# A first scan spread over twelve tiles, a second scan whose last half states and transposes come one tile later, and router steps woven into the gate products

## The chip, the core and the metric

The kernel runs on one core of a Trainium2 chip. The metric is the device time of one execution in microseconds (us), and less is better. TensorE is called PE here (its weight loads PEld), VectorE is DVE, ScalarE is ACT, GpSimd is POOL, and SP is the engine that issues most DMAs.

## What is computed

The input x is 1024 rows of 256 (4 sequences of 256). It passes a feed-forward layer with experts, a state-space scan, and the same feed-forward layer again, each behind a layer norm:

```python
x = x + 0.5 * ffn(layernorm(x))
x = x + ssm(layernorm(x))
x = x + 0.5 * ffn(layernorm(x))

def ffn(x):            # 8 routed experts, top 2 by sigmoid score; 2 shared experts; hidden width 640
    scores = sigmoid(x @ w_router.T)
    w, i = top_k(scores, 2); w = w / w.sum()
    routed = sum over the 2 chosen experts of w * (silu(x @ wg.T) * (x @ wu.T)) @ wd.T
    return routed + the same without a weight for the 2 shared experts

def ssm(x):            # 256 channels, 16 states each
    proj = x @ W_xproj.T; dt = softplus(proj[:256]); B, C = proj[256:272], proj[272:]
    h[t] = exp(dt * A) * h[t-1] + dt * B * x;  y[t] = sum over states of h[t] * C + D * x
```

All arithmetic is in float32.

## The kernel before

The 1024 rows are taken as two halves of 512, and the two feed-forward layers over two halves make four **segments** 0 to 3. A segment has 17 **tiles** of 128 rows, numbered through from 0 to 67 (`LIST`, with S1 = 17, S2 = 34 and S3 = 51 the first tiles of segments 1 to 3). Of the 17, eight are "shared" (the two shared experts, four row blocks each), five are "whole" (routed experts 0 to 4, 128 slots each), and four are "mixed" (four groups of 32 rows, each with an expert of its own, one of which is read from a table). Shared tiles that are in the set `DIRECT` take their input from `xnt`, the transposed normed rows in SBUF. All other tiles fetch 128 rows from DRAM (`xg_rows`) four tiles ahead on SP's queue, and PE turns them two tiles ahead (`rows_of`, L560), after which ACT copies them to `xt` (L786).

Every engine walks one table, `SCHEDULE`, in order. A tile n is done in two steps. `first(n)` issues the ten gate and up products of tile **n+1** (chunks of 128 columns: `gate_up(n+1)` 0 to 4, 4 to 8, and then 8 to 10, which waits until tile n-1 has been evicted). `second(n)` turns the rows of tile n+2 and issues the down product of tile n (L541, L554). On ACT `first` is the tanh of tile n+1 (L768), and for a mixed tile before it the copy of its turned hidden rows; `second` is the copy to `xt` and, for routed tiles, the eviction (L793), and behind it `send_late(n)` sends expert weights (L802). On DVE `first` is `hidden(n+1)` (L1017 and L1021), and `second` is the eviction of a shared tile into `xres` (L1032). `("tiles", a, b)` is both steps for each of a to b-1, and in `("scan", a, b, h)` the half states of scan h are added to each tile.

A **scan** h (one half of 512 rows) has 32 **half states**: 16 states times two blocks of 128 channels. For each, ACT makes the decay (L858, L859), POOL the input `bx` (L981), DVE the scan itself (L1062) and the product with C (L1067), and POOL adds that to the sum in `xnt` (L995). There are two buffers of each kind, one for each channel block. `half_states(first, n, part)` says which of them stand ahead of (part 0) and behind (part 1) tile n's body: two ahead and one behind, with two at the first tile of a scan. `("X1", h)` projects the scan's inputs ahead of it, and `("Y", h)` turns the finished sum back (L738), once the last add is done.

The **router** of a segment is four steps: R1 (logits, 16 matmuls of 32 rows, L694), a copy by DVE and its transpose on PE (`turn_logits`, L596), `route_scores` on DVE (L1103 to L1122, the top two), R2 (two matmuls that count ranks, L703, L704), and `route_rows` on DVE (L1127 to L1167, the place of every row). The step S then scatters rows from POOL (L943), G gathers results (L961), C adds them to `xres` (L1175), and N1, N2 and T are the layer norm (P before a feed-forward layer, A before a scan) and its transposes (L684).

Weights: shared expert 0 comes first on SP's queue; shared expert 1 and routed expert 0 (`EARLY`) follow there in the step "start". Experts 1 to 7 are sent from ACT's queue behind the tiles that `LATE` names. The first mixed tile of segment 0 has every expert in it, so `first_use` lets PE wait for the gate and up weights of all eight before its gate products:

```python
                if kind_of(n) == "mixed":
                    if index_of(n) == 0:
                        for e in range(E):
                            weights_in(e, k)
```

## Time and profile before

| | |
|---|---|
| median of 3 runs | 530.93 us (530.12 to 531.57) |
| the profiled execution | 526.55 us |
| its span, first to last instruction | 524.8 us |
| PE busy | 509.9 us (97%) |
| DVE busy | 324.4 us (62%) |
| POOL busy | 231.3 us (44%) |
| ACT busy | 158.3 us (30%) |
| data moved by DMA | 67.76 MB |

The span is the profiled execution without what lies around it; the execution's own time is 1.75 us longer. Busy shares are over the whole span, while the stages differ: the two scans fill DVE and POOL, and the rest leaves them half idle. In the timeline a row gives start, length, engine, line, operation, names, shape and count of the instructions merged in it, and in brackets the idle time ahead of the first and what ended it. A float32 matmul shows as two passes, so that a chunk with its two halves of the contraction counts as x4.

### The profile page before, as it was taken

To read this page: it belongs to the slowest core of one execution; us is meant where nothing else is said; L and a number is where in the kernel's file an instruction comes from. 1 tells how busy PE (TensorE), PEld (TensorE's weight loads), DVE (VectorE), ACT (ScalarE), POOL (GpSimd) and SP (SyncE) were. 2 spreads that over 40 slices of the span, in tenths; PEclk is the share of its full clock that TensorE was granted. 3 is DMA by queue.
4 is the path that set the end of the run, shared out by engine and by line. 5 is a ranking of instruction groups with operands and counts; after the bars stand their busy time and mean duration, and the time that the engine had idled before them with its cause. 6 is when DMAs were issued, how large, how long until landed. Compare 5 with 4: busy or idle time off the path is not lost.

```text
span 524.8 us, 11147 instructions
## 1 busy us (share of the span) xinstructions
PE 509.9 (97%) x4408; PEld 413.2 (79%) x4409; DVE 324.4 (62%) x658; ACT 158.3 (30%) x336; POOL 231.3 (44%) x208
## 2 busy tenths in 40 slices
PE   7999999999999999899999999999999999999996
PEld 6899997448988888347998889974479999954696
DVE  3742526521665999998698399999867522522225
ACT  1111121222036444453213643554431111122210
POOL 1050100220513999996445389999900650000041
PEclk9999999999999999999999999999999999999999
DMA  7967995931303455540312525545100231210022
GB/s 225 372 245 275 400 397 206 330 97 31 93 23 134 114 134 157 143 139 23 107 56 92 132 94 125 132 145 152 52 12 14 80 102 41 81 40 15 19 62 72
DMA packets 42087, 67.76 MB, mean 129 GB/s; under 512 B 5136, under 2 KB 24848, under 8 KB 42032
## 3 DMA queue, kind: packets, MB, share of 16 engines
q1 hardware_dynamic: 29280, 38.81, 25.7%
q10 hardware_dynamic: 9088, 18.09, 9.3%
q0 software_dynamic: 3664, 10.10, 6.0%
q8 instruction: 37, 0.61, 0.5%
q14 instruction: 18, 0.15, 0.1%
HBM read 48.76 MB, written 18.22 MB: 128 GB/s over the span
## 4 chain that ended last, share of the span: by engine, by line
PE 65%; POOL 12%; DVE 9%; issue 7%; DMA 5%; SPq 1%; POOLq 0%; ACT 0%; DVEq 0%
PE ps L516 29%; PE ps L541 13%; PE ps L531 11%; POOL region L981 8%; PE ps L554 7%; POOL xnt L995 4%; DVE ps L1062 3%; DMA bcb<-bc_rows 2%; PE ps L565 2%; DMA w_gu<-in_su 1%; PE ps L560 1%; DMA bc_rows<-hh 1%; DVE hb L1017 1%; PE ps L684 1%; DVE xres L1175 1%
## 5 line engine op out<-in xcount | busy, mean ns | idle before, releaser
L516 PEld LDWEIGHTS ps<-xt,w_gu 128*128 128x128 f32 x1360 | 156.6, 192 | 12.6 <-ACT xt L786 4.9
L516 PE MATMUL ps<-xt,w_gu 128*128 128x128 f32 x1360 | 162.3, 277 | 2.5 <-DVE xres L1032 1.5
L1017 DVE SCALAR_TENSOR_TENSOR hb<-hb,ps 128x640 f32<-128x640 f32 x68 | 55.5, 816 | 128.9 <-ACT hb L768 128.7
L541 PE MATMUL ps<-w_dn,hb 128*128 128x256 f32 x520 | 120.7, 379 | 0.0
L541 PEld LDWEIGHTS ps<-w_dn,hb 128*128 128x128 f32 x520 | 94.9, 190 | 10.8
L768 ACT ACTIVATE hb<-ps 128x640 f32<-128x640 f32 x68 | 47.5, 699 | 171.4 <-PE ps L516 157.0
L516 PEld LDWEIGHTS ps<-xnt,w_gu 128*128 128x128 f32 x720 | 82.9, 192 | 1.9 <-issue 1.2
L516 PE MATMUL ps<-xnt,w_gu 128*128 128x128 f32 x720 | 84.1, 276 | 0.2 <-DMA w_gu<-in_su 0.2
L995 POOL TENSOR_TENSOR xnt<-xnt,hh 128x512 f32<-128x512 f32 x64 | 82.6, 1293 | 1.3 <-DVE hh L1067 1.3
L1062 DVE TENSOR_TENSOR_SCAN ps<-ps,region 128x512 f32<-128x512 f32 x64 | 78.2, 1223 | 7.5 <-POOL region L981 7.4
L961 POOL DMA_INDIRECT region<-yg_rows,ypos x32 | 30.6, 956 | 109.4 <-DMA yg_rows<-ob 87.3
L531 PE MATMUL ps<-w_gu,xt 128*32 128x512 f32 (+2 forms) x768 | 74.4, 524 | 2.3 <-ACT xt L786 1.6
L943 POOL DMA_INDIRECT xg_rows<-region,pos x32 | 31.5, 983 | 87.3 <-DVE pos L1159 35.1
L981 POOL TENSOR_TENSOR region<-region,bcb 128x512 f32<-128x512 f32 x44 | 56.6, 1289 | 19.0 <-DMA bcb<-bc_rows 16.4
L1021 DVE TENSOR_TENSOR hb<-hb,ps 128x640 f32<-128x640 f32 x68 | 55.8, 821 | 2.3
L531 PEld LDWEIGHTS ps<-w_gu,xt 128*32 128x32 f32 x768 | 23.0, 109 | 42.3 <-issue 38.4
L859 ACT ACTIVATE ps<-region,aneg 128x510 f32<-128x510 f32 x64 | 43.2, 676 | 0.0
L554 PE MATMUL ps<-w_dn,hb 128*32 128x256 f32 (+1 forms) x640 | 37.6, 380 | 0.0
L858 ACT ACTIVATE ps<-pre 128x2 f32<-128x2 f32 x64 | 11.1, 173 | 69.0 <-DVE hh L1067 69.0
L1067 DVE TENSOR_TENSOR hh<-ps,bcb 128x512 f32<-128x512 f32 x44 | 30.4, 691 | 1.5
L554 PEld LDWEIGHTS ps<-w_dn,hb 128*32 128x32 f32 x640 | 20.3, 110 | 13.6 <-issue 0.8
L793 ACT ACTIVATE ob<-ps 128x256 f32<-128x256 f32 x36 | 13.8, 383 | 53.4 <-PE ps L554 34.0
(111 smaller groups left out, 315.0 us busy)
## 6 DMA issues: line engine op xcount, KB each, us to landing
bcb<-bc_rows SPq DMA_DIRECT2D x22, 512.0 KB, 5.1
region<-bc_rows SPq DMA_DIRECT2D x10, 512.0 KB, 5.4
w_gu<-in_wg ACTq DMA_DIRECT2D x7, 640.0 KB, 8.3
w_gu<-in_wu ACTq DMA_DIRECT2D x7, 640.0 KB, 9.9
w_dn<-in_wd ACTq DMA_DIRECT2D x7, 640.0 KB, 10.9
xg<-xg_rows SPq DMA_DIRECT2D x34, 128.0 KB
yg_rows<-ob SPq DMA_DIRECT2D x20, 128.0 KB, 4.3
xg_rows<-bcb SPq DMA_DIRECT2D x1, 2176.0 KB, 14.9
```

The costliest lines, as they stand in the source:

```text
L516: last = nc.tensor.matmul(gup(p)[:, c * P:(c + 1) * P], w_gu4[:, e, k, c * P:(c + 1) * P], x, start=(k == 0), stop=(k == KC - 1))
L531: last = nc.tensor.matmul(gup(p)[r:r + GROUP, a:b], xt[:, p, k, r:r + GROUP], w, start=(k == 0), stop=(k == KC - 1))
L541: ins = nc.tensor.matmul(outp(p), hb[:, p, c * P:(c + 1) * P], w_dn4[:, e, c, :], start=(c == 0), stop=(c == IC - 1))
L554: ins = nc.tensor.matmul(outp(p)[r:r + GROUP, :], hb[:, p, c * P + r:c * P + r + GROUP], w, start=(c == 0), stop=(c == IC - 1))
L768: nc.scalar.activation(hb[:, p, :], gup(p)[:, 0:I], ACT.Tanh, scale=0.5).then_inc(s_tanh, 1)
L859: nc.scalar.activation(bank[:, :, 1:L], dt[:, d, :].rearrange("p (b t) -> p b t", b=2)[:, :, 1:L], ACT.Exp, scale=aneg[:, d * N + m:d * N ...
L943: nc.gpsimd.indirect_dma_start(out=xg_dram[s % 2], out_offset=bass.IndirectOffsetOnAxis(ap=pos[:, s, j, t:t + 1], axis=0), in_=xn["P"][:, ...
L981: nc.gpsimd.tensor_tensor(bx[:, d, :], dtx[:, d, :], bcs[m % SLOTS][:, 0, :], ALU.mult).then_inc(s_bx, 1)
L995: nc.gpsimd.tensor_tensor(xnt[:, d, :], xnt[:, d, :], hh[:, d, :], ALU.add).then_inc(s_acc, 1)
L1017: nc.vector.scalar_tensor_tensor(out=h, in0=h, scalar=1.0, in1=gup(p)[:, 0:I], op0=ALU.add, op1=ALU.mult).then_inc(s_a, 1)
L1021: nc.vector.tensor_tensor(h, h, gup(p)[:, I:GU], ALU.mult).then_inc(s_h, 1)
L1062: nc.vector.tensor_tensor_scan(state_banks[:, d, :], state_banks[:, d, :], bx[:, d, :], 0.0, ALU.mult, ALU.add).then_inc(s_scan, 1)
```

## The change

1. **Segment 0** has one tile of the second shared expert ahead of its routed tiles rather than two, so that the whole tiles are 5 to 9 and the mixed ones 10 to 13, and three shared tiles follow. `DIRECT[0]` loses tile 5, which now is routed. `LATE` sends experts 5 and 6 behind tile 5 and expert 7 behind tile 6.
2. **The first scan** begins at tile S1+1 instead of S1+2, with all that stands ahead of it one tile earlier (the gather, the combining, the norm, X1), and ends at the same tile. Its 32 half states are given by `SHARES`: 2 or 3 a tile over twelve tiles, all but one of them ahead of the body.
3. **The second scan** still begins at S2+2, but spreads its half states over twelve tiles, to S2+13, and Y, N1 and N2 for the last segment come behind the whole of that tile instead of between its two steps. T comes behind tile S2+14's second step.
4. **The router**: in segment 0 the logits stand behind two chunks of the first tile's gates instead of ahead of all, and their transpose behind six instead of four. In all segments the two rank matmuls stand behind the first four chunks of the following tile's gates (`ranked`) instead of ahead of them; `route_rows` still stands ahead of `hidden` on DVE. In segment 3 the logits come behind four chunks and their transpose behind eight (`routed`) instead of ahead of all and behind four. The sign flip of the decay rates (`decay`) is a step of its own.

```diff
--- before.py
+++ after.py
@@ -45,7 +45,7 @@
 
 SHARED = [[("shared", E + k, t) for t in range(TT)] for k in range(NSH)]
 ROUTED = [("whole", e, e) for e in range(WHOLE)] + [("mixed", None, m) for m in range(MT)]
-ORDERS = [SHARED[0] + SHARED[1][:2] + ROUTED + SHARED[1][2:],
+ORDERS = [SHARED[0] + SHARED[1][:1] + ROUTED + SHARED[1][1:],
           SHARED[0] + SHARED[1][:1] + ROUTED + SHARED[1][1:],
           SHARED[0] + SHARED[1][:2] + ROUTED + SHARED[1][2:],
           SHARED[0] + ROUTED + SHARED[1]]
@@ -55,7 +55,7 @@
 LIST = [tile for order in ORDERS for tile in order]
 
 
-DIRECT = [set(range(TT + 2)), {0, 1}, {0, 1}, {j for j in range(SEG_TILES) if ORDERS[3][j][0] == "shared"}]
+DIRECT = [set(range(TT + 1)), {0, 1}, {0, 1}, {j for j in range(SEG_TILES) if ORDERS[3][j][0] == "shared"}]
 
 
 def kind_of(n):
@@ -111,11 +111,10 @@
 
 def half_states(first, n, part):
 
-    a = PER_TILE * (n - first) - 1
-    a, b = (a, a + 2) if part == 0 else (a + 2, a + PER_TILE)
-    if n == first:
-        a, b = (0, 0) if part == 0 else (0, 2)
-    return range(a, b)
+    share = SHARES[segment(first) - 1]
+    a, count = sum(share[:n - first]), share[n - first]
+    ahead = 0 if n == first else count - 1
+    return range(a, a + ahead) if part == 0 else range(a + ahead, a + count)
 
 
 def slot_loads(h, m):
@@ -123,26 +122,27 @@
 
 
 HALVES = KC * N
-PER_TILE = 3
+SHARES = [[2, 2, 3, 2, 3, 3, 2, 3, 3, 3, 3, 3], [2, 3, 3, 2, 3, 3, 2, 3, 3, 3, 3, 2]]
 SLOTS = 3
 
 
 
 S1, S2, S3 = SEG_TILES, 2 * SEG_TILES, 3 * SEG_TILES
 SCHEDULE = [
-    ("N1", "P", 0), ("N2", "P", 0), ("T", "P", 0), ("R1", 0), ("start",), ("R2", 0), ("S", 0, 0), ("S", 0, 1),
-    ("tiles", 0, 6), ("N1", "P", 1), ("N2", "P", 1), ("tiles", 6, 8), ("T", "P", 1), ("tiles", 8, 9), ("R1", 1),
-    ("scored", 9, 1), ("second", 9), ("R2", 1), ("S", 1, 0), ("S", 1, 1), ("tiles", 10, S1 - 2), ("O", 0), ("G", 0),
-    ("tiles", S1 - 2, S1 - 1), ("C", 0, 0, 2), ("tiles", S1 - 1, S1), ("C", 0, 2, 3), ("first", S1), ("C", 0, 3, TT),
-    ("N1", "A", 0), ("second", S1), ("N2", "A", 0), ("first", S1 + 1), ("T", "A", 0), ("second", S1 + 1), ("X1", 0),
-    ("scan", S1 + 2, S1 + 13, 0), ("first", S1 + 13), ("Y", 0), ("N1", "P", 2), ("N2", "P", 2), ("second", S1 + 13),
+    ("N1", "P", 0), ("N2", "P", 0), ("T", "P", 0), ("start",), ("ranked", 0, 0), ("S", 0, 0), ("S", 0, 1),
+    ("second", 0), ("tiles", 1, 6), ("N1", "P", 1), ("N2", "P", 1), ("tiles", 6, 8), ("T", "P", 1), ("tiles", 8, 9), ("R1", 1),
+    ("scored", 9, 1), ("second", 9), ("ranked", 10, 1), ("decay",), ("S", 1, 0), ("S", 1, 1),
+    ("second", 10), ("tiles", 11, S1 - 3), ("O", 0), ("G", 0),
+    ("tiles", S1 - 3, S1 - 2), ("C", 0, 0, 2), ("tiles", S1 - 2, S1 - 1), ("C", 0, 2, 3), ("first", S1 - 1),
+    ("C", 0, 3, TT), ("second", S1 - 1), ("N1", "A", 0), ("N2", "A", 0), ("first", S1), ("T", "A", 0), ("second", S1),
+    ("X1", 0), ("scan", S1 + 1, S1 + 13, 0), ("first", S1 + 13), ("Y", 0), ("N1", "P", 2), ("N2", "P", 2), ("second", S1 + 13),
     ("O", 1), ("G", 1), ("first", S1 + 14), ("T", "P", 2), ("second", S1 + 14), ("R1", 2),
-    ("scored", S1 + 15, 2), ("second", S1 + 15), ("R2", 2), ("S", 2, 0), ("tiles", S2 - 1, S2), ("C", 1, 0, TT), ("N1", "A", 1),
+    ("scored", S1 + 15, 2), ("second", S1 + 15), ("ranked", S2 - 1, 2), ("S", 2, 0), ("second", S2 - 1), ("C", 1, 0, TT), ("N1", "A", 1),
     ("S", 2, 1), ("tiles", S2, S2 + 1), ("N2", "A", 1), ("first", S2 + 1), ("T", "A", 1), ("second", S2 + 1), ("X1", 1),
-    ("scan", S2 + 2, S2 + 13, 1), ("first", S2 + 13), ("Y", 1), ("N1", "P", 3), ("N2", "P", 3), ("second", S2 + 13),
-    ("first", S2 + 14), ("T", "P", 3), ("second", S2 + 14), ("O", 2), ("R1", 3),
-    ("scored", S2 + 15, 3), ("second", S2 + 15), ("R2", 3), ("S", 3, 0), ("S", 3, 1), ("G", 2),
-    ("tiles", S2 + 16, S3 + 6), ("C", 2, 0, TT), ("tiles", S3 + 6, S3 + 13), ("O", 3), ("G", 3),
+    ("scan", S2 + 2, S2 + 14, 1), ("Y", 1), ("N1", "P", 3), ("N2", "P", 3), ("first", S2 + 14),
+    ("second", S2 + 14), ("O", 2), ("T", "P", 3), ("routed", S2 + 15, 3), ("second", S2 + 15), ("ranked", S2 + 16, 3),
+    ("S", 3, 0), ("S", 3, 1), ("G", 2),
+    ("second", S2 + 16), ("tiles", S3, S3 + 6), ("C", 2, 0, TT), ("tiles", S3 + 6, S3 + 13), ("O", 3), ("G", 3),
     ("tiles", S3 + 13, TILES - 2), ("C", 3, 0, 2), ("first", TILES - 2), ("C", 3, 2, TT), ("second", TILES - 2),
     ("tiles", TILES - 1, TILES),
 ]
@@ -353,7 +353,7 @@
 
 
         EARLY = (E + 1, 0)
-        LATE = {3: (1, 2), 4: (3, 4), 5: (5,), 6: (6,), 7: (7,)}
+        LATE = {3: (1, 2), 4: (3, 4), 5: (5, 6), 6: (7,)}
 
         def weights_of(e):
 
@@ -591,12 +591,30 @@
                         pe.wait_ge(s_ev, n - 1)
                     gate_up(n, free[n], 8, 2 * IC).then_inc(s_up, 1)
 
+            def score(s):
+                pe.wait_ge(s_xnt, 2 * (NORM["P", s] + 1))
+                for d in range(KC):
+                    for t in range(TT):
+                        last = nc.tensor.matmul(bank6[t * GROUP:(t + 1) * GROUP, 0:P], wr[:, d, :],
+                                                xnt[:, d, t * P:(t + 1) * P], start=(d == 0), stop=(d == KC - 1))
+                last.then_inc(s_lg, 1)
+                held[:] = []
+
+            def rank(s):
+                pe.wait_ge(s_oh, s + 1)
+                banks_free()
+                flat = both[:, :, :].rearrange("p t e -> p (t e)")
+                nc.tensor.matmul(bank7[:, 0:TT * E], upper[:, :], flat, start=True, stop=True)
+                nc.tensor.matmul(bank7[:, TT * E:2 * TT * E], ones[:, :], flat, start=True,
+                                 stop=True).then_inc(s_rk, 1)
+                held[:] = [(s_rkc, s + 1)]
+
             def turn_logits(s):
                 pe.wait_ge(s_lgc, s + 1)
                 nc.tensor.transpose(bank6[:, P:2 * P], turned_logits, ident[:, :]).then_inc(s_lg, 1)
                 held[:] = [(s_neg, s + 1)]
 
-            def first(n, router=None):
+            def first(n, router=None, ranks=None, both_steps=False):
                 q = n % 2
                 if n + 1 < TILES:
                     first_use(n + 1, 0)
@@ -606,13 +624,20 @@
                     free[n + 1] = free_expert(segment(n + 1), index_of(n + 1)) if kind_of(n + 1) == "mixed" else None
                     gate_up(n + 1, free[n + 1], 0, 4)
                 if router is not None:
-                    turn_logits(router)
+                    if both_steps:
+                        score(router)
+                    else:
+                        turn_logits(router)
+                if ranks is not None:
+                    rank(ranks)
                 if kind_of(n) == "mixed":
                     pe.wait_ge(s_h, n + 1)
                     turn_hidden(hb[:, q, :], hidden_turned(q)).then_inc(s_tr6, 1)
                     rows_of(n)
                 if n + 1 < TILES:
                     gate_up(n + 1, free[n + 1], 4, 8).then_inc(s_gate, 1)
+                if both_steps:
+                    turn_logits(router)
                 rest_of_gate_up(n + 1)
 
             def second(n):
...
+                    pe.wait_ge(s_xnt, 2 * NORM["P", 0] + 1)
+                    gate_up(0, None, 0, 2)
+                    score(0)
+                    gate_up(0, None, 2, 6)
                     turn_logits(0)
-                    gate_up(0, None, 4, 8).then_inc(s_gate, 1)
+                    gate_up(0, None, 6, 8).then_inc(s_gate, 1)
                     gate_up(0, None, 8, 2 * IC).then_inc(s_up, 1)
                 elif kind == "X1":
                     h = step[1]
...
@@ -901,6 +917,11 @@
                     first(step[1])
                 elif kind == "scored":
                     exponentials(step[2])
+                    first(step[1])
+                elif kind == "routed":
+                    first(step[1])
+                    exponentials(step[2])
+                elif kind == "ranked":
                     first(step[1])
                 elif kind == "second":
                     second(step[1])
@@ -1073,6 +1094,8 @@
                     for t in range(TT):
                         ins = nc.vector.bn_stats(st[:, t, :], src[:, t, :])
                     link(ins)
+                else:
+                    link(nc.vector.bn_stats(st[:, TT - 1, :], src[:, TT - 1, :]))
                 for t in range(TT):
                     ins = nc.vector.bn_aggr(mv[:, t, :], st[:, t, :])
                 link(ins)
@@ -1182,7 +1205,7 @@
                         else:
                             ins.then_inc(s_comb, 1)
                             dve.wait_ge(s_comb, TT * s + t + 1)
-                if s < 2:
+                if s < 2 and t1 < TT:
                     link(nc.vector.bn_stats(st[:, t1 - 1, :], x[:, t1 - 1, :]))
 
             nc.vector.memset(zeros, 0.0).then_inc(s_zero, 1)
...
@@ -1256,6 +1278,13 @@
                 elif kind == "scored":
                     route_scores(step[2])
                     first(step[1])
+                elif kind == "routed":
+                    copy_logits(step[2])
+                    route_scores(step[2])
+                    first(step[1])
+                elif kind == "ranked":
+                    route_rows(step[2])
+                    first(step[1])
                 elif kind == "second":
                     second(step[1])
                     done = step[1] + 1
```

Three places where the rows move. First **PE, the start of the program** (L694 and after it L598 are the logits; L596, then L614, their transpose; L703 and L704, then L607 and L608, the ranks; L516 the gate and up products, two matmuls a chunk). Before, and then after:

```order
L684 MATMUL ps<-ident,region 128x128 x8
L694 MATMUL ps<-xnt,wr 32x128 x8
L516 MATMUL ps<-xnt,w_gu 128x128 x8
L596 MATMUL ps<-ident,hh 128x128
L516 MATMUL ps<-xnt,w_gu 128x128 x12
L703 MATMUL ps<-both,upper 128x32
L704 MATMUL ps<-both,ones 128x32
L516 MATMUL ps<-xnt,w_gu 128x128 x20
L541 MATMUL ps<-w_dn,hb 128x256 x5
```

```order
L709 MATMUL ps<-ident,region 128x128 x8
L516 MATMUL ps<-xnt,w_gu 128x128 x4
L598 MATMUL ps<-xnt,wr 32x128 x8
L516 MATMUL ps<-xnt,w_gu 128x128 x8
L614 MATMUL ps<-ident,hh 128x128
L516 MATMUL ps<-xnt,w_gu 128x128 x16
L607 MATMUL ps<-both,upper 128x32
L608 MATMUL ps<-both,ones 128x32
L516 MATMUL ps<-xnt,w_gu 128x128 x12
L541 MATMUL ps<-w_dn,hb 128x256 x5
```

The logits now wait for two chunks, the transpose stands two chunks later, and the ranks four chunks deep in tile 1's gates.

Second **ACT, tiles 3 and 4, where the late weights are first sent** (L768, then L784, is the tanh of the next tile; L786, then L802, the copy of turned rows to `xt`; L802, then L818, the weight transfers). Before, and then after:

```order
L864 ACTIVATE ex<-ex 128x32
L768 ACTIVATE hb<-ps 128x640 x5
L802 DMA w_gu<-in_wg 128x2x640
L802 DMA w_gu<-in_wu 128x2x640
L802 DMA w_dn<-in_wd 128x1280
```

```order
L880 ACTIVATE ex<-ex 128x32
L784 ACTIVATE hb<-ps 128x640 x5
L802 ACTIVATE xt<-ps 128x256
L818 DMA w_gu<-in_wg 128x2x640
L818 DMA w_gu<-in_wu 128x2x640
L818 DMA w_dn<-in_wd 128x1280
```

The first weights of routed expert 1 now stand behind the copy of tile 5's turned rows, for which ACT waits on PE.

Third **DVE, the end of the second scan** (L1062, then L1083, is the scan; L1067, then L1088, the product with C; L1017 and L1021, then L1038 and L1042, `hidden`; L1237, then L1259, adds the turned sum behind Y). Before, and then after:

```order
L1062 SCALAR_TENSOR_TENSOR ps<-ps,region 128x512
L1067 TENSOR_TENSOR hh<-ps,bcb 128x512
L1017 SCALAR_TENSOR_TENSOR hb<-hb,ps 128x640
L1021 TENSOR_TENSOR hb<-hb,ps 128x640
L1062 SCALAR_TENSOR_TENSOR ps<-ps,region 128x512
L1067 TENSOR_TENSOR hh<-ps,bcb 128x512
L1017 SCALAR_TENSOR_TENSOR hb<-hb,ps 128x640
L1021 TENSOR_TENSOR hb<-hb,ps 128x640
L1237 TENSOR_TENSOR xres<-xres,ps 128x512 x2
```

```order
L1083 SCALAR_TENSOR_TENSOR ps<-ps,region 128x512
L1088 TENSOR_TENSOR hh<-ps,bcb 128x512
L1038 SCALAR_TENSOR_TENSOR hb<-hb,ps 128x640
L1042 TENSOR_TENSOR hb<-hb,ps 128x640
L1083 SCALAR_TENSOR_TENSOR ps<-ps,region 128x512
L1088 TENSOR_TENSOR hh<-ps,bcb 128x512
L1259 TENSOR_TENSOR xres<-xres,ps 128x512 x2
```

The last half state now stands behind the `hidden` of the last mixed tile (S2+14) instead of ahead of it.

## Rows read from the trace of the kernel before

**Rows 1.** The page: busy time, share of the span and instructions of each engine.

```profile
PE 509.9 (97%) x4408; PEld 413.2 (79%) x4409; DVE 324.4 (62%) x658; ACT 158.3 (30%) x336; POOL 231.3 (44%) x208
```

**Rows 2.** Timeline of PE: the gates of two tiles that fetch rows, outside the scans.

```profile
59.07 4.63 PE L516 MATMUL ps<-xt,w_gu 128*128 128x128 f32 x40
...
65.91 4.63 PE L516 MATMUL ps<-xt,w_gu 128*128 128x128 f32 x40
```

**Rows 3.** Windows: stretch, length, busy PE, PEld, DVE, ACT, POOL, PE clock, DMA.

```profile
158.74:246.62 87.88, 85.30 (x758) 64.99 (x757) 79.74 (x93) 44.82 (x107) 79.19 (x64) 1.00 0.46 125
...
292.37:380.67 88.30, 85.18 (x722) 64.93 (x721) 79.97 (x94) 43.99 (x105) 79.20 (x64) 1.00 0.48 123
```

**Rows 4.** Timeline of DVE and POOL inside the first scan.

```profile
202.55 1.22 DVE L1062 TENSOR_TENSOR_SCAN ps<-ps,region 128x512 f32<-128x512 f32 x1
...
204.41 0.81 DVE L1017 SCALAR_TENSOR_TENSOR hb<-hb,ps 128x640 f32<-128x640 f32 x1
...
206.00 1.22 DVE L1062 TENSOR_TENSOR_SCAN ps<-ps,region 128x512 f32<-128x512 f32 x1
...
195.68 1.27 POOL L981 TENSOR_TENSOR region<-region,bcb 128x512 f32<-128x512 f32 x1
...
198.14 1.27 POOL L981 TENSOR_TENSOR region<-region,bcb 128x512 f32<-128x512 f32 x1
```

**Rows 5.** Timeline of PE: the two waits at the first mixed tiles, first scan.

```profile
210.45 4.50 PE L531 MATMUL ps<-w_gu,xt 128*32 x48 [0.80 <-ACT xt L786]
...
220.48 0.76 PE L565 MATMUL ps<-ident,hb 128*128 128x128 f32 x5 [0.94 <-DVE hb L1021]
```

**Rows 6.** Timeline of PE and DVE at the start.

```profile
12.29 2.02 PE L516 MATMUL ps<-xnt,w_gu 128*128 128x128 f32 x16 [0.17 <-DMA w_gu<-in_su]
14.15 0.27 PE L596 MATMUL ps<-ident,hh 128*128 128x128 f32 x1
...
18.33 0.41 PE L703 MATMUL ps<-both,upper 128*128 128x32 f32 x2 [1.23 <-DVE both L1116]
...
25.50 4.63 PE L516 MATMUL ps<-xnt,w_gu 128*128 128x128 f32 x40
...
28.23 0.42 DVE L1032 SCALAR_TENSOR_TENSOR xres<-ps,xres 128x256 f32<-128x256 f32 x1
```

**Rows 7.** Weights: timeline of ACT's queue and PE, one transfer's landing, one window.

```profile
42.61 0.69 ACTq L802 DMA_DIRECT2D w_gu<-in_wg  x1
...
43.22 2.32 PE L541 MATMUL ps<-w_dn,hb 128*128 128x256 f32 x10
...
73.54 0.63 ACTq L802 DMA_DIRECT2D w_gu<-in_wu  x1
...
w_gu<-in_wu ACTq DMA_DIRECT2D x1, 640.0 KB, 9.9
...
81.14 2.05 PE L516 MATMUL ps<-xt,w_gu 128*128 128x128 f32 x16
...
89.12 4.50 PE L531 MATMUL ps<-w_gu,xt 128*32 x48 [0.39 <-issue]
...
43.00:83.00 40.00, 40.00 (x314) 37.92 (x313) 15.22 (x33) 7.95 (x16) 1.89 (x2) 1.00 1.02 386
```

**Rows 8.** Timeline of POOL: the last add of the second scan.

```profile
378.67 1.28 POOL L995 TENSOR_TENSOR xnt<-xnt,hh 128x512 f32<-128x512 f32 x1 [0.63 <-DVE hh L1067]
```

**Rows 9.** Timeline of PE and DVE at the router of the last segment.

```profile
394.91 0.27 PE L596 MATMUL ps<-ident,hh 128*128 128x128 f32 x1
...
406.93 4.63 PE L516 MATMUL ps<-xnt,w_gu 128*128 128x128 f32 x40
...
409.33 0.42 DVE L1032 SCALAR_TENSOR_TENSOR xres<-ps,xres 128x256 f32<-128x256 f32 x1
```

**Rows 10.** Windows over PE's filling matmuls at the start, columns as in rows 3.

```profile
2.00:4.00 2.00, 2.00 (x6) 1.53 (x6) 0.00 (x0) 0.03 (x1) 0.00 (x0) 1.00 0.84 257
6.00:8.00 2.00, 2.00 (x10) 1.73 (x10) 0.83 (x6) 0.00 (x0) 0.95 (x1) 1.00 0.93 321
```

38 lines of the change are left out of this document (12 added, 26 removed).

## The prediction

> **What bounds the kernel now.** I read four views, in this order. The page: PE is busy 97% of the span [rows 1], so what can be won is PE's waits and what stretches its work. The timeline of PE: a tile that fetches its rows costs PE 65.91 - 59.07 = 6.84 us outside the scans [rows 2]; a direct tile, which turns no rows, costs 6.63 (in segment 0 the gates of tile 2 start at 25.50 and the down product of tile 3 at 43.22, two such tiles and ten chunks of 0.446 us apart [rows 6, 7]). The windows: each scan lasts 88 us, in which DVE is busy for 80 and POOL for 79 [rows 3]. Last DVE and POOL inside a scan: a half state takes DVE 204.41 - 202.55 = 1.86 us, `hidden` 206.00 - 204.41 = 1.59, and an eviction of a shared tile another 0.33, while POOL needs 198.14 - 195.68 = 2.46 a half state [rows 4]. A tile with three half states therefore takes DVE 3 x 1.86 + 1.59 = 7.17, or 7.50 with an eviction, and PE, with 6.84, follows DVE. In the first scan three tiles of the second kind lose 0.66 each and four of the first kind 0.33 each, and two more waits of 0.80 and 0.94 stand at the first mixed tiles, since a mixed tile wants its hidden rows earlier [rows 5]: 2.0 + 1.3 + 1.7 = 5.0 us. The second scan has one more tile with an eviction and a late start: some 6.
>
> **First scan.** With twelve tiles two of the first three tiles have two half states, and two later ones. DVE's tile costs 5.64 with two and an eviction, 5.31 with two and none. Summed over `SHARES`, DVE's need up to the first mixed tile is 2 x 5.64 + 7.50 + 5.64 + 4 x 7.17 + 5.31 = 58.4 for nine tiles against PE's 9 x 6.84 = 61.6, so that DVE no longer stretches PE, and comes to the mixed tiles in time. POOL needs 32 x 2.46 = 78.7 us plus some 9 ahead of its steady run, and PE now takes about 90 for the stretch up to Y, so the last add is in time. One wait of some 0.3 stays at the start, where the first load of B and C is awaited. I take a gain of 4.6; the bounds are 2.5 (POOL or ACT's copy to `xt` still hold PE at some tiles) and 5.0.
>
> **Second scan.** The stretch starts where it did, and POOL's chain is as long: its last add ends at 378.67 + 1.28 = 379.95 now [rows 8], 0.7 ahead of Y at 380.67 [rows 3]. In the change one more `hidden` (1.59) stands ahead of the last half state, and it has to wait for PE's gates of tile S2+14; so the last add comes at about 381.7 to 382. PE without DVE's stretching would be through the whole of tile S2+13 some 2.7 us before that, and waits in Y. Before, tile S2+13's down product (2.3 us) followed Y; now it is done. So Y ends at 382.9, where before Y and that down product ended at 383.99, by adding 2.3 and Y's 1.0 to 380.67: the gain is 1.1, not 6. Bounds: -1 and +3. What is late next is the last add of POOL, with PE idle in front of L750.
>
> **Start.** The transpose of the logits moves from 14.15 to 12.29 + six chunks (2.7) + the logits (0.6) = 15.55, so DVE's router is 1.4 later. PE saves part of its wait of 1.23 at the ranks [rows 6]: it comes there at 19.2 and waits until 19.7. But DVE's queue has `route_rows` ahead of `hidden(1)` and the eviction of tile 0, which ends at 28.23 + 0.42 = 28.65 now and at 30.05 then; PE wants it for the last two chunks of tile 2, 3.6 after 25.50, that is at 29.1 now and at 28.8 then. So PE waits 1.3 and is **1.0 later** than before. Bounds: -0.3 (the eviction in time) and +1.4.
>
> **Tile 5 is routed.** One more tile is turned: +0.2. Its rows are wanted at 43.22 + 1.0 on PE; the scatter is up to 1.4 later than before. I take +0.2, bounds 0 and 1.4.
>
> **Weights, the largest term.** From 43 to 83 the DMA engines move 386 GB/s at a share of 1.02: they are full for 40 us [rows 7]. The last of the gate and up weights, those of expert 7, are issued at 73.54 and land 9.9 later, at 83.4; PE wants them at 89.12 and does not wait. In the change the first mixed tile is tile 10, whose gates stand at 81.14 now, then at 81.14 + 1.0 + 0.2 = 82.3. That alone is a wait of 1.1. And the stream starts later: the first transfer goes out at 42.61, with the last tanh before it; then it stands behind the copy of tile 5's turned rows, which PE turns at 44.2, so it goes out at about 44.65, 2.05 later. A full queue hands that on one for one, and two more transfers of 128 KB (tile 5's rows in and out) add 0.65 at that rate. Expert 7 lands at 83.4 + 2.05 + 0.65 = 86.1, and PE waits 3.7. That `LATE` sends experts 5 to 7 a tile sooner changes nothing in a queue that is full. Bounds: 1.1 (the stream makes up its late start) and 4.5.
> The Trainium skill, Perfetto Trace Analysis, section Roofline, has 16 DMA engines move up to some 435 GB/s together. By that figure the 40 us of transfers would shrink by 4.5 us, an estimate from that page, and PE would hardly wait at all; this trace shows 386 at full share.
>
> **Ranks and logits inside the gates.** In segments 1 and 2 no wait stood at the ranks, so nothing is saved there, and `route_rows` starts later against PE: between 0 and 1.8 (four chunks) each. Behind it PE waits for `hidden(11)` and, in segment 2, for the combining and the norm that fill DVE without a gap. I take 0.8 for both. In segment 3 the transpose comes four chunks (1.8) later. From it to the end of tile S2+16's eviction DVE takes 409.33 + 0.42 - 394.91 = 14.8; PE wants that eviction 406.93 + 3.6 - 394.91 = 15.6 after the transpose [rows 9], and 13.8 after it in the change. Wait: 1.0, and 0.3 more since ACT has the tanh ahead of the router's exponential. I take +1.3, bounds 0 and 1.8.
>
> **Sum**, against the profiled execution's own 526.55: +1.0 +0.2 +0.2 +3.7 +0.8 +1.3 - 4.6 - 1.1 = +1.5, which gives 528.05. The median of the runs, 530.93, is 4.4 above that execution, so the same change on it gives **532.4 us**. A measurement of this kernel can tell about 0.3% (1.6 us) from no change; the forecast lies at that edge.
>
> **Rivals.**
> *The weights come in time.* If what keeps the queue busy is not the engines' limit but how it is fed, the earlier issue of experts 5 to 7 pays, and PE finds expert 7 there: the term of 3.7 goes, and the sum is -2.2, 528.7 us: faster. The point from which it decides is a landing before 82.3. For it speaks no row. Against it: a share of 1.02 over 40 us [rows 7]. 0.17. (The page named above, with its 435 GB/s, would have it so.)
> *PE's clock falls in its wait.* The filling matmuls at the start begin six in 2 us at first and ten in 2 us later [rows 10], so PE runs at 1.2 GHz after idleness and then at 2.4; in those first 4.3 us it does half the work. The longest wait in the rows after that is 1.23 us [rows 6], and the granted clock stays at 1.00. A wait of 3.7 could bring the low level back; once, that costs 2.2 more: 534.6 us. The Trainium skill, TensorE: Matmul & The Clock Gate, section on HAM oscillation, has an array that waits for DMA fall back to the low clock; no wait of this length is in this trace. 0.13.
> *The scans gain less.* If POOL's steady 2.46 or ACT's chain of exponentials ahead of the tanh holds PE as before, the first scan gives 2.5 and the second nothing: 535.6 us. For it: POOL has no gap in the last 60 us of either scan. Against: twelve tiles of PE work are longer than POOL's sum. 0.12.
> *It does what it is meant to at the router but the waits behind DVE are not there*, because DVE's slack is larger than my sums: start, ranks and segment 3 give nothing, 529.3 to 530 us, no change to the eye. 0.08.
>
> **How the numbers follow.** My forecast (the sum within its smaller bounds, 530.9 to 534) has 0.50, half of it beyond 532.5. Faster by over 0.3%: most of the first rival, 0.15. Slower by over 0.3%: 0.26 of the forecast, the clock and the scans, 0.51. The rest, 0.34, is within 0.3%. The range reaches from the first rival's 528.7 to just short of the scans' 535.6: 528.9 to 535.4.
>
> **What would show it.** Right: ahead of the gates of tile 10 (L531, about 82 us) PE idle some 3 to 4 us behind a weights transfer of expert 7, and the DMA share at 1.0 until about 86; PE idle 2 to 3 us ahead of L750 in the second scan behind POOL's L1016; inside the first scan a spacing of 6.8 to 6.9 us where there was 7.2 to 7.5; short waits behind DVE's eviction (L1053) near 29 us and in tile S3+1. Wrong: no wait at tile 10, a granted clock below 1, or gates in the first scan still 7.2 us apart.

## The result, and the profile after

The changed kernel takes **536.6 us** (median of 4 runs, 535.2 to 538.9) where the kernel before, run beside it, takes 531.2: a ratio of 1.010, with a 95% interval of 1.0074 to 1.0126. It is 5.4 us slower. The prediction was 532.4 with a range of 528.9 to 535.4: the direction was right, the size was not. The profiled execution of the change is one of 536.17, with a span of 534.4.

On some occasions everything takes about 4.5 us longer, on one and the same chip too (the kernel before took 530.9 and 531.3 on two of them and 526.6 and 526.3 on two others, and its profile shown ahead of the prediction is one of 526.55), so that ratios are taken to the kernel before on the same occasion. Both kernels were therefore profiled once more side by side. There the kernel before is 526.6 (span of the profile 524.5) and the changed one 534.5 (median of 5, 530.96 to 536.3; its profiled execution is the quickest, 530.96, span 529.2): a ratio of 1.017, from 1.0152 to 1.0187 (the quotient of the two medians is 1.015).

The page of the change, busy time and the clock's row; below it windows of it, columns as in [rows 3]. [Rows 1] had PE at 509.9 us, and its clock was full throughout.

```profile
PE 512.6 (96%) x4410; PEld 417.6 (78%) x4411; DVE 324.2 (61%) x658; ACT 158.8 (30%) x337; POOL 231.8 (43%) x208
...
PEclk9999989999999999999999999999989999999999
```

```profile
69.46:72.88 3.42, 3.42 (x19) 3.42 (x17) 0.67 (x1) 0.00 (x0) 0.00 (x0) 0.50 1.04 415
390.32:393.73 3.41, 3.41 (x18) 3.41 (x17) 3.04 (x11) 0.00 (x0) 0.19 (x1) 0.50 0.02 5
```

PE is busy all through both stretches and does half the work: 1.7 us are lost in each. What stands ahead of them shows in the timeline of PE, with the other waits over 1 us behind the first 2 us (the kernel before had no wait over 1 us at any of these places, [rows 6, 7] and Y at 380.67):

```profile
29.16 1.16 PE L516 MATMUL ps<-xnt,w_gu 128*128 128x128 f32 x8 [1.25 <-DVE xres L1053]
...
68.84 6.33 PE L516 MATMUL ps<-xt,w_gu 128*128 128x128 f32 x40 [2.36 <-ACT xt L802]
...
87.07 1.92 PE L531 MATMUL ps<-w_gu,xt 128*32 x16 [1.23 <-issue]
...
289.51 1.16 PE L516 MATMUL ps<-xt,w_gu 128*128 128x128 f32 x8 [1.06 <-DVE xres L1053]
...
389.43 1.17 PE L750 MATMUL ps<-ident,xnt 128*128 128x128 f32 x8 [4.51 <-POOL xnt L1016]
390.39 3.55 PE L516 MATMUL ps<-xt,w_gu 128*128 128x128 f32 x16
...
420.02 1.16 PE L516 MATMUL ps<-xnt,w_gu 128*128 128x128 f32 x8 [1.01 <-DVE xres L1053]
```

The wait of 2.36 at the gates of tile 8 was in no part of the prediction. Its releaser is ScalarE's copy to `xt`; the timeline of ScalarE and its queue says why that copy is late:

```profile
61.59 0.55 ACTq L818 DMA_DIRECT2D w_gu<-in_wg  x1
62.17 0.63 ACTq L818 DMA_DIRECT2D w_gu<-in_wu  x1
62.84 4.78 ACTq L818 DMA_DIRECT2D w_dn<-in_wd  x1
67.71 0.70 ACT L784 ACTIVATE hb<-ps 128x640 f32<-128x640 f32 x1 [7.66 <-issue]
67.79 1.17 ACTq L818 DMA_DIRECT2D w_gu<-in_wg  x1
68.31 0.38 ACT L802 ACTIVATE xt<-ps 128x256 f32<-128x256 f32 x1
```

`LATE` sends experts 5 and 6 together behind tile 5. The last of those six issues takes 4.78 us where the others take 0.6, and the tanh of the next tile and the copy to `xt` stand behind it on ScalarE. Of the 17 transfers ahead of it in this stream nine were still on the way when it began and six when it was let go. The four other issues of this trace over 1 us (1.07 to 2.19) began with seven or eight on the way; but one that began with eight took 0.63, so that the number alone does not tell which issue is held. It is not SP's queue that holds it: SP's own two issues in that time (64.35 and 64.73) took 0.35 and 0.43.

The wait at tile 10 is not for weights either in this execution: the last of them, expert 7's `wu`, landed at 84.36, and PE came there at 85.84. In the quicker profile (span 529.2) it landed at 84.23 and PE came at 83.66, so that 0.57 of the wait of 1.78 is weights and 1.2 is PE's own queue (below).

**Where the difference lies, on one occasion.** The start of the down product of seven tiles on PE in the two profiles taken side by side, the kernel before first, then the change (timelines of PE):

```profile
63.49 2.32 PE L541 MATMUL ps<-w_dn,hb 128*128 128x256 f32 x10
130.86 2.32 PE L541 MATMUL ps<-w_dn,hb 128*128 128x256 f32 x10
170.33 2.32 PE L541 MATMUL ps<-w_dn,hb 128*128 128x256 f32 x10
238.54 2.34 PE L554 MATMUL ps<-w_dn,hb 128*32 x40
296.51 2.32 PE L541 MATMUL ps<-w_dn,hb 128*128 128x256 f32 x10
397.40 2.32 PE L541 MATMUL ps<-w_dn,hb 128*128 128x256 f32 x10
411.10 2.32 PE L541 MATMUL ps<-w_dn,hb 128*128 128x256 f32 x10
```

```profile
63.91 2.32 PE L541 MATMUL ps<-w_dn,hb 128*128 128x256 f32 x10
135.63 2.32 PE L541 MATMUL ps<-w_dn,hb 128*128 128x256 f32 x10
175.29 2.32 PE L541 MATMUL ps<-w_dn,hb 128*128 128x256 f32 x10
239.14 2.34 PE L554 MATMUL ps<-w_dn,hb 128*32 x40
297.57 2.32 PE L541 MATMUL ps<-w_dn,hb 128*128 128x256 f32 x10
400.64 2.32 PE L541 MATMUL ps<-w_dn,hb 128*128 128x256 f32 x10
415.76 2.32 PE L541 MATMUL ps<-w_dn,hb 128*128 128x256 f32 x10
```

These are tiles 6, 15, 20, 29, 36, 49 and 51. The change is behind by 0.42, 4.77, 4.96, 0.60, 1.06, 3.24 and 4.66 us, which makes a ledger beside the prediction's terms:

| stretch | predicted | in the trace |
|---|---|---|
| start (tiles 0 to 2) | +1.0 | +0.21 |
| tile 5 routed, its rows | +0.4 | +0.21 |
| tile 8, ScalarE held up | none | +2.29 |
| tile 10, weights and PE's own queue | +3.7 | +2.06 |
| ranks in segments 1 and 2 | +0.8 | +0.19 +0.46 |
| first scan (tiles 20 to 29) | -4.6 | -4.36 |
| second scan and Y (tiles 36 to 49) | -1.1 | +2.18 |
| router of segment 3 | +1.3 | +1.42 |
| sum | +1.5 | +4.66 |

In this quickest execution the clock fell once, behind Y (3.41 us at half, 1.7 of the +2.18). The other four have mean clocks of 0.989 to 0.993 where this one has 0.995; 0.001 of the mean is 0.53 us, so that by this estimate 1 to 3 of their 3 to 5 us more are further stretches at half clock. What the rest of it is stays open: there is one profile.

### The profile page after: what moved, and what is told of

Same layout as the page of the kernel before. It is cut to its first block, busy times and chain, and to the rows that moved or that the text cites. A ratio compares the mean times of both kernels' runs of the same rounds, so it can differ in the third digit from the quotient of the medians.

```text
span 534.4 us, 11154 instructions
## 1 busy us (share of the span) xinstructions
PE 512.6 (96%) x4410; PEld 417.6 (78%) x4411; DVE 324.2 (61%) x658; ACT 158.8 (30%) x337; POOL 231.8 (43%) x208
## 4 chain that ended last, share of the span: by engine, by line
PE 73%; DVE 14%; DMA 4%; issue 3%; ACTq 1%; POOL 1%; ACT 1%; SPq 1%; another core or an unknown queue 0%; DVEq 0%; POOLq 0%
PE ps L516 32%; PE ps L541 16%; PE ps L531 13%; PE ps L554 6%; DVE ps L1083 2%; DMA bcb<-bc_rows 2%; PE ps L560 2%; DVE hb L1038 2%; PE ps L565 2%; ACTq L818 1%; DMA w_gu<-in_su 1%; DVE hb L1042 1%; DMA bc_rows<-hh 1%; PE ps L709 1%; DVE xres L1198 1%
## 5 line engine op out<-in xcount | busy, mean ns | idle before, releaser
L516 PEld LDWEIGHTS ps<-xt,w_gu 128*128 128x128 f32 x1400 | 165.0, 195 | 10.4 <-issue 5.7
L516 PE MATMUL ps<-xt,w_gu 128*128 128x128 f32 x1400 | 168.3, 279 | 4.1 <-ACT xt L802 2.4
L1038 DVE SCALAR_TENSOR_TENSOR hb<-hb,ps 128x640 f32<-128x640 f32 x68 | 55.5, 816 | 123.1 <-ACT hb L784 107.3
L784 ACT ACTIVATE hb<-ps 128x640 f32<-128x640 f32 x68 | 47.6, 701 | 185.5 <-PE ps L516 163.0
L516 PE MATMUL ps<-xnt,w_gu 128*128 128x128 f32 x680 | 81.0, 276 | 3.3 <-DVE xres L1053 3.0
L1083 DVE TENSOR_TENSOR_SCAN ps<-ps,region 128x512 f32<-128x512 f32 x64 | 78.3, 1223 | 9.2 <-POOL region L1002 6.4
L516 PEld LDWEIGHTS ps<-xnt,w_gu 128*128 128x128 f32 x680 | 79.0, 192 | 5.8 <-DVE xres L1053 3.6
L1042 DVE TENSOR_TENSOR hb<-hb,ps 128x640 f32<-128x640 f32 x68 | 55.8, 821 | 4.1 <-DVE hb L1038 1.2
L554 PE MATMUL ps<-w_dn,hb 128*32 128x256 f32 (+1 forms) x640 | 38.8, 380 | 0.7 <-issue 0.6
L554 PEld LDWEIGHTS ps<-w_dn,hb 128*32 128x32 f32 x640 | 21.4, 110 | 14.6 <-issue 2.1
L1088 DVE TENSOR_TENSOR hh<-ps,bcb 128x512 f32<-128x512 f32 x44 | 30.4, 691 | 1.5
L943 POOL TENSOR_TENSOR rs<-ve,mhalf 128x4 f32<-128x4 f32 x6 | 6.2, 1040 | 47.8 <-DVE ve L1102 47.8
```

The lines of the kernel that those rows point to most:

```text
L516: last = nc.tensor.matmul(gup(p)[:, c * P:(c + 1) * P], w_gu4[:, e, k, c * P:(c + 1) * P], x, start=(k == 0), stop=(k == KC - 1))
L554: ins = nc.tensor.matmul(outp(p)[r:r + GROUP, :], hb[:, p, c * P + r:c * P + r + GROUP], w, start=(c == 0), stop=(c == IC - 1))
L784: nc.scalar.activation(hb[:, p, :], gup(p)[:, 0:I], ACT.Tanh, scale=0.5).then_inc(s_tanh, 1)
L1038: nc.vector.scalar_tensor_tensor(out=h, in0=h, scalar=1.0, in1=gup(p)[:, 0:I], op0=ALU.add, op1=ALU.mult).then_inc(s_a, 1)
L1042: nc.vector.tensor_tensor(h, h, gup(p)[:, I:GU], ALU.mult).then_inc(s_h, 1)
L1083: nc.vector.tensor_tensor_scan(state_banks[:, d, :], state_banks[:, d, :], bx[:, d, :], 0.0, ALU.mult, ALU.add).then_inc(s_scan, 1)
```

## The experiments

### What holds the start of the weights

```diff
-        LATE = {3: (1, 2), 4: (3, 4), 5: (5, 6), 6: (7,)}
+        LATE = {3: (1, 2), 4: (3, 4), 5: (5,), 6: (6,), 7: (7,)}
```

> The changed kernel with LATE as in the kernel before: experts 5, 6 and 7 sent one per tile, behind tiles 5, 6 and 7. Theory A (ScalarE is held up while it issues a transfer into a queue that is full, and so its copy to xt for tile 8 is late): no issue of L818 takes over 1.1 us, the wait of 2.36 us ahead of the gates of tile 8 is gone and so is the half clock behind it; but the weights then are what is late, and the first mixed tile, tile 10, waits some 3 us for expert 7 (landing about 84.6, wanted about 81.7). If a wait of 3 us brings the clock down as those of 2.36 and 4.51 did, the total gains only some 0 to 1 us: 535.6 to 536.6. Rival B (the weights come in time if nothing blocks): no wait at tile 10 either, 532.5. Rival C (the rows of tile 8 are late whoever issues, because the DMA engines are full): the wait of 2.4 at tile 8 stays, 536.6.

Measured: 539.3 us, 1.0155 times before (1.0133 to 1.0177): 2.7 slower than the change. The copy to `xt` is in time (64.28, and PE's gates of tile 8 start 4.3 us sooner), so theory A holds for tile 8 and rival C is out. But the wait at tile 10 is not 3:

```profile
80.90 0.65 PE L598 MATMUL ps<-xnt,wr 128*32 128x128 f32 x16
87.27 3.28 PE L531 MATMUL ps<-w_gu,xt 128*32 x16 [5.73 <-issue]
```

Expert 7's `wu` is issued at 73.87 and lands 12.2 later, at 86.1, and 1.2 us of PE's own queue (below) follow. In the change it was issued at 68.98 and landed 15.4 later, at 84.4. So sending experts 5 and 6 together did bring the last weights 1.7 us sooner, and the whole wait moved: 2.36 at tile 8 and 1.23 at tile 10, or 5.73 at tile 10, with the low clock behind either. Of the 2.7 us only some 1.5 belong to this (the lag behind the change at tile 9); another 1.2 came behind Y, where the clock stayed at half for 6.83 us here and for 3.41 in the change. "No issue over 1.1 us" did not come true: three took 2.91, 1.20 and 1.86, but none of them had a copy that PE waited for behind it.

```diff
-        LATE = {3: (1, 2), 4: (3, 4), 5: (5, 6), 6: (7,)}
+        LATE = {2: (1,), 3: (2, 3), 4: (4,), 5: (5,), 6: (6,), 7: (7,)}
```

> The changed kernel with the stream of late weights started one tile earlier: LATE = {2: (1,), 3: (2, 3), 4: (4,), 5: (5,), 6: (6,), 7: (7,)}. Theory A (ScalarE's blocked issue and the late start of the stream are the two causes of the waits at tiles 8 and 10): no issue over 1.1 us, waits of 2.36 and the half clock at tile 8 gone, expert 7 lands by about 81 and the first mixed tile waits only for PE's own sequencer (0.4 to 1.2): 4.0 to 4.9 us less, 531.7 to 532.6. Rival: the DMA engines were busy before 42 us with the router's rows, and those are now late: a new wait at the gates of tile 5 or 6 of 1 us and more, 533.5 or above.

Measured: 538.7 us, ratio 1.0142 (1.0121 to 1.0163). The rival was right: the wait at tile 10 is down to 1.20, but PE waits 2.82 for the rows of tile 5 at 47.09, and its clock falls at 48.40. The router's scatter shares the DMA engines with expert 1 here (their share from 40 to 42 us is 1.01, and 0.16 in the change), and the fetch of the rows, which waits for it, goes out at 44.9 and not at 40.7.

### The last half state

```diff
-    ahead = 0 if n == first else count - 1
+    ahead = 0 if n == first else count if first > S2 and n - first == len(share) - 1 else count - 1
```

> The changed kernel with both half states of the second scan's last tile ahead of that tile's step on ScalarE and VectorE, none behind it. Theory A (the last half state stands behind ScalarE's copy of the down product, so Y can't start before PE is through and the exponential, scan, product and POOL's add have followed one after another): the wait of 4.51 ahead of Y (L750) falls to about 0.6, the clock stays full behind it: 3.9 + 1.7 = 5.6 less, 531.0. Rival B (my prediction's: POOL's chain of 2.46 a half state is what ends last): the last add comes no more than 1.8 sooner, a wait of 2.7 stays and the clock still falls: 534.8; or without the fall 533.1.

Measured: 531.6 us (12 runs), ratio 1.0016 (1.0000 to 1.0031), 5.0 less than the change; theory A, rival B is out. The wait and the low clock behind it are gone (PE's timeline):

```profile
386.54 1.09 PE L750 MATMUL ps<-ident,xnt 128*128 128x128 f32 x8 [0.79 <-POOL xnt L1016]
387.47 1.95 PE L516 MATMUL ps<-xt,w_gu 128*128 128x128 f32 x16
```

The chain that was cut stands in the timelines of the change (the profile of 530.96) like this: ScalarE evicts the down product of tile S2+13, and only then makes the decay of the last half state; VectorE waits for that, POOL for VectorE, PE for POOL.

```profile
379.73 0.38 ACT L809 ACTIVATE ob<-ps 128x256 f32<-128x256 f32 x1 [1.98 <-PE ps L554]
380.01 0.17 ACT L874 ACTIVATE ps<-pre 128x2 f32<-128x2 f32 x1
380.10 0.68 ACT L875 ACTIVATE ps<-region,aneg 128x510 f32<-128x510 f32 x1
380.82 1.23 DVE L1083 TENSOR_TENSOR_SCAN ps<-ps,region 128x512 f32<-128x512 f32 x1 [1.64 <-ACT ps L875]
382.08 0.69 DVE L1088 TENSOR_TENSOR hh<-ps,bcb 128x512 f32<-128x512 f32 x1
382.85 1.26 POOL L1016 TENSOR_TENSOR xnt<-xnt,hh 128x512 f32<-128x512 f32 x1 [3.70 <-DVE hh L1088]
384.17 1.83 PE L750 MATMUL ps<-ident,xnt 128*128 128x128 f32 x8 [4.51 <-POOL xnt L1016]
```

POOL itself is idle for 3.70 us ahead of its last add: it is not POOL's chain that ends last, as [rows 8] had it before.

```diff
-SHARES = [[2, 2, 3, 2, 3, 3, 2, 3, 3, 3, 3, 3], [2, 3, 3, 2, 3, 3, 2, 3, 3, 3, 3, 2]]
+SHARES = [[2, 2, 3, 2, 3, 3, 2, 3, 3, 3, 3, 3], [2, 3, 3, 3, 3, 3, 3, 3, 3, 3, 3]]
-    ("scan", S2 + 2, S2 + 14, 1), ("Y", 1), ("N1", "P", 3), ("N2", "P", 3), ("first", S2 + 14),
+    ("scan", S2 + 2, S2 + 13, 1), ("first", S2 + 13), ("Y", 1), ("N1", "P", 3), ("N2", "P", 3), ("second", S2 + 13), ("first", S2 + 14),
```

> The changed kernel with the second scan as in the kernel before: eleven tiles, Y between the two parts of the tile behind them. Theory A (the new second scan gains nothing: what its tiles save, the wait at Y takes, and on top PE's clock halves for one stretch): the stretch from the first gates of the scan to the first shared gates behind Y and the down product is as long as in the kernel before, 91.6 us, and the half clock at 390 is gone: 1.7 to 2.0 less, 534.7. Rival B (the new second scan gains 1.1 as predicted, and the half clock is all that it loses): 0.6 less, 536.0.

Measured: 535.0 us, ratio 1.0070 (1.0049 to 1.0092), 1.7 less than the change; the two intervals overlap, so the traces have to decide. From the down product of tile 36 to that of tile 49 it takes 404.98 - 303.94 = 101.04 us, and the change 405.88 - 303.19 = 102.69: the difference of 1.65 is what the half clock costs (1.7), and nothing is left over. So the new second scan, as it is put, gains nothing at all over the old; with the last half state ahead it gains 3.7 (97.30 us for the same stretch in e3_ahead). This profile has another fall of the clock, outside the stretch and with no long wait ahead of it: from 11.86 to 15.27 us it is at half, behind two waits of 0.71 and 0.93 at the start.

```profile
9.48 1.32 PE L709 MATMUL ps<-ident,region 128*128 128x128 f32 x8 [0.71 <-DVE region L1115]
11.72 1.92 PE L516 MATMUL ps<-xnt,w_gu 128*128 128x128 f32 x8 [0.93 <-DMA w_gu<-in_su]
```

### The first scan

```diff
-SHARES = [[2, 2, 3, 2, 3, 3, 2, 3, 3, 3, 3, 3], ...
+SHARES = [[2, 3, 3, 3, 3, 3, 3, 3, 3, 3, 3, 0], ...
```

> The changed kernel with the first scan's half states spread as in the kernel before, two in the first tile and three in each of the next ten, none in the twelfth. Theory A (VectorE's tile of three half states, 7.17 or 7.50 with an eviction, holds PE, whose tile is 6.84): the tiles of the scan are 7.2 to 7.5 apart again with waits of 0.8 and 0.9 at the first mixed tiles, and the gain of the first scan, 4.5, is lost: 541. Rival (the gain came from the extra tile having work of PE's that stood elsewhere before, not from the spreading): within 1 us of the changed kernel.

Measured: 538.0 us, ratio 1.0212 (1.0193 to 1.0231) where the change has 1.0170 (1.0152 to 1.0187) on an occasion of this kind: 2.2 us slower by the ratios, 3.5 by the medians, and 5.9 by the traces (in the stretch from tile 18's down product to tile 27's). Why the times of the runs differ by less than the traces is not shown; the expectation had 4.5. The tiles stand 7.15 and 7.17 apart again, and the two waits of [rows 5] are back as 0.80 and 1.14:

```profile
191.96 2.32 PE L541 MATMUL ps<-w_dn,hb 128*128 128x256 f32 x10
...
199.11 2.32 PE L541 MATMUL ps<-w_dn,hb 128*128 128x256 f32 x10
...
206.28 2.32 PE L541 MATMUL ps<-w_dn,hb 128*128 128x256 f32 x10
```

These are tiles 22 to 24. In the change they start at 188.98, 195.82 and 202.66, 6.84 apart. The spreading is what the first scan gains by.

### Curing the waits

Both cures together, the last half state ahead and another `LATE`, which uses that the DMA engines are little used from 32 to 44 us of the change (its window 36 to 40, columns as in [rows 3]):

```profile
36.00:40.00 4.00, 4.00 (x29) 3.74 (x28) 2.07 (x3) 0.70 (x1) 2.62 (x3) 1.00 0.33 115
```

```diff
-        LATE = {3: (1, 2), 4: (3, 4), 5: (5, 6), 6: (7,)}
+        LATE = {1: (1,), 3: (2, 3), 4: (4,), 5: (5,), 6: (6,), 7: (7,)}
```

> The changed kernel with the last half state ahead, as in e3_ahead, and with expert 1's weights sent behind tile 1, into the 12 us in which the DMA engines are idle: LATE = {1: (1,), 3: (2, 3), 4: (4,), 5: (5,), 6: (6,), 7: (7,)}. Theory A (the stream has 5 us less to move behind tile 3, ScalarE never meets a full queue, and the router's scatter is done with by then): no issue of L818 over 1.2 us, no wait at tile 8, full clock throughout, at tile 10 only the 1.2 us of PE's sequencer; 4.2 less than e3_ahead, 527.4. Rival: the scatter of tile 5's rows is late as in e2_early, a wait at tile 5 of 1 to 3 us, with the half clock if it is over 2: 529 to 532.

Measured: 529.3 us, **0.9964** times before (0.9951 to 0.9978), 2.8 less than with the first cure alone. Tile 8 waits no more and the clock is full throughout; of the 4.4 won there, 1.6 go to the rival, a wait for the rows of tile 5 that is too short here to bring the clock down:

```profile
45.04 0.41 PE L560 MATMUL ps<-ident,xg 128*128 128x128 f32 x2 [1.60 <-DMA xg<-xg_rows]
```

On this kernel, the router steps. Ranks of segments 1 to 3 ahead of the gates again:

```diff
-    ("second", 9), ("ranked", 10, 1), ("decay",), ("S", 1, 0), ("S", 1, 1), ("second", 10), ("tiles", 11, S1 - 3),
+    ("second", 9), ("R2", 1), ("decay",), ("S", 1, 0), ("S", 1, 1), ("tiles", 10, S1 - 3),
...
-    ("ranked", S2 - 1, 2), ("S", 2, 0), ("second", S2 - 1),
+    ("R2", 2), ("S", 2, 0), ("tiles", S2 - 1, S2),
...
-    ("ranked", S2 + 16, 3), ("S", 3, 0), ("S", 3, 1), ("G", 2), ("second", S2 + 16), ("tiles", S3, S3 + 6),
+    ("R2", 3), ("S", 3, 0), ("S", 3, 1), ("G", 2), ("tiles", S2 + 16, S3 + 6),
```

> e5_cured with the ranks in segments 1 to 3 as in the kernel before, ahead of the tile's gates and not inside them. Theory A (my prediction's term: VectorE's rows of the router begin four chunks later against PE and its evictions are late by as much): the waits of 0.8 and 1.06 at the end of segment 1 fall to the 0.5 of before, the wait of 1.01 in tile S3+1 goes; 2.0 less than e5_cured. Rival B (VectorE's work is the bound at these places wherever the ranks stand, or the ranks now wait for VectorE's scores): within 0.5 of e5_cured, with a wait ahead of the ranks.

Measured: 529.2 us, ratio 0.9959 (0.9946 to 0.9972): rival B. The waits behind VectorE's evictions (0.78 at 279, 1.01 in tile S3+1) become waits at the ranks (0.73 and 1.10), and that of 1.06 at 287 stays: it is VectorE's work that lies on the path there, wherever the ranks stand. The logits and the transpose of segment 3 (`routed`) stay where the change has them in this kernel and in all that follow.

The start as before, and both:

```diff
-    ("N1", "P", 0), ("N2", "P", 0), ("T", "P", 0), ("start",), ("ranked", 0, 0), ("S", 0, 0), ("S", 0, 1), ("second", 0), ("tiles", 1, 6),
+    ("N1", "P", 0), ("N2", "P", 0), ("T", "P", 0), ("R1", 0), ("start",), ("R2", 0), ("S", 0, 0), ("S", 0, 1), ("tiles", 0, 6),
```

> e5_cured with the start as in the kernel before: logits, four chunks, transpose, ranks behind tile 0's gates, then tile 0. Theory A (the new start begins its gates 1.2 us sooner and gives the same back in the wait of 1.25 behind VectorE at 29 us): within 0.5 of e5_cured, the wait at 29 gone, one of 1.2 at the ranks in its place. Rival (my prediction's term of 1.0): 1.0 less than e5_cured.

> e5_cured with both edits of e6 and e7: only the twelve-tile scans, the routed step of segment 3 and the weights are other than before. Expected: the sum of both, 2.0 less than e5_cured by theory A of e6, equal to it by rival B.

Measured: 528.7 us, 0.9954 (0.9939 to 0.9969), and 528.7, 0.9951 (0.9937 to 0.9965). Each is within 0.7 of e5_cured, and no interval tells them apart. By the traces the old start is 0.3 sooner at tile 1; the wait of 1.25 at 29 goes and one of 1.23 at the ranks is there, as theory A had it.

Last, PE's own queue. Ahead of the first mixed tile it waits for two transfers of each of eight experts, though it has waited for experts 0 to 4 already:

```diff
-                        for e in range(E):
+                        for e in range(WHOLE, E):
                             weights_in(e, k)
```

> e8_cured_all with PE waiting ahead of the first mixed tile for the weights of experts 5 to 7 alone (those of 0 to 4 it has waited for in the tiles before): 6 waits in its queue and not 16. Theory A (the 1.20 ahead of the gates of tile 10 is PE's own sequencer, which takes 0.107 us a wait and stands behind the 32 instructions of the logits): ten waits, 1.07 less, so the pause is 0.1 to 0.4 and the total 0.9 less than e8_cured_all. Rival (it is the load of the free expert's number from the table, 0.55, and what follows it, with the waits hidden): the pause stays at 1.2. The pauses of 0.2 and 0.8 in the down products of the mixed tiles stay in both.

Measured: 523.3 us on an occasion of 526.6, ratio 0.9934 (0.9918 to 0.9951). The pause fell from 1.20 to 0.70, half of what theory A expected; what is left is the rival's cause: in this trace PE's queue takes the load of the number from 82.45 to 82.95, and the steps that make the address of it until 83.42. Each wait takes 0.106 there, but about half of what the ten take stood behind the logits' matmuls and cost nothing. The kernel once more, on the occasion of the two profiles of the ledger:

> e11_six_waits, unaltered, on the same chip as the three above: 0.9934 times e12 again, 3.3 to 3.5 less than the kernel before, 0.5 from the six waits.

Measured: **523.9 us, 0.9952 times before (0.9939 to 0.9964)**, with 526.6 for the kernel before and 534.5 for the change on the same occasion. So this version beats both; against e8_cured_all (0.9951) the six waits are worth 0.5 by the pause, and nothing that the ratios could show.

### What halves the clock

```diff
                     h = step[1]
+                    for _ in range(18 * h):
+                        nc.tensor.matmul(gup((S2 + 13) % 2)[:, 0:H], ones[:, :], w_gu4[:, 0, 0, 0:H], start=True, stop=True)
                     pe.wait_ge(s_acc, (h + 1) * HALVES)
```

> The changed kernel with 18 matmuls of ones ahead of Y's wait in the second scan, into a bank that nobody uses then (they compute nothing that is used): 18 x 0.216 = 3.9 us of work in PE's wait of 4.51. Theory A (the clock halves because PE is idle): PE's wait ahead of L750 is 0.6, the grant stays full at 390, the shared gates behind Y take 2.0 and not 3.55: 1.7 less than the changed kernel, 534.9. Rival (the clock falls there for another reason, such as what PE did in the 100 us before): half clock again behind the fill, 536.6 or above.

Measured: 534.7 us, ratio 1.0155 (1.0134 to 1.0177). The clock stays full behind Y, but each of my matmuls is two instructions, so that the fill lasts 7.8 us and holds Y up by 3.3 itself (its row: 381.58, x36, 8.04 us). With half as many, side by side with both kernels unaltered:

> The kernel before, unaltered, with a profile from the same chip as that of the next run. The chips differ: the kernel before took 531 on one and 526.6 on another. Theory A (one chip adds pauses at fixed instructions of PE, in the down products of the mixed tiles and behind the logits, whatever the kernel): where this run takes 531, its profile has pauses of 0.3 to 0.8 in L554 of segment 0 that its first profile, of 526.55, had not, and VectorE sees the logits of segment 2 late; where it takes 526.6 it has none. Rival: the 4.4 us are spread over everything, each tile 0.06 longer.

> The changed kernel, unaltered. Theory A: 1.0101 times e12, 5.4 more, whichever the chip, within 1 us, with the waits of 2.4 and 4.5 and the half clock behind the second. Rival (the chip's pauses fall into waits of one kernel and not of the other): on the chip of 526.6 the changed kernel is some 7 to 8 over e12, since e9_fill_y and e10_old_shares were 8.1 and 11.4 over it.

> As e9_fill_y with 9 matmuls and not 18: each took 0.43 us there and not the 0.216 that I had taken, so that 18 filled 7.8 us. 9 x 0.43 = 3.9 us in a wait of 4.51. Theory A (idleness halves the clock): wait ahead of Y 0.6, full clock behind it, 1.7 less than e13. Rival: half clock all the same, equal to e13.

Measured: 526.6 for the kernel before (ratio to its other runs on that occasion 1.0008), 534.5 for the change (1.0170), and 532.0 with the fill (1.0110, from 1.0096 to 1.0125), 2.5 less than the change. Timeline of PE with the fill, then a window behind Y:

```profile
382.29 4.15 PE L747 MATMUL ps<-w_gu,ones 128*128 128x256 f32 x18
386.87 1.09 PE L752 MATMUL ps<-ident,xnt 128*128 128x128 f32 x8 [0.42 <-POOL xnt L1018]
387.79 1.95 PE L516 MATMUL ps<-xt,w_gu 128*128 128x128 f32 x16
```

```profile
387.80:391.20 3.40, 3.40 (x33) 3.40 (x32) 3.00 (x11) 0.59 (x1) 0.22 (x1) 1.00 0.02 5
```

Y begins when it would have, and the gates behind it take 1.95 and not 3.55: it was PE's idleness that brought the clock down, and 1.65 us between the down products on either side of Y are won by work that computes nothing. (The medians differ by 0.9 more than that, for which no cause is shown; the fall at tile 8 is in this profile, behind a wait of 2.52, and not in that of the change.) The rival of e13 came true by its number: the change is 7.8 over the kernel before here and 5.4 over it in the first result. Its cause is not shown. These are five and four executions that lie 5.4 and 3.6 us apart, and the profiled one is here only 4.7 over that of the kernel before.

As to theory A of e12, the traces of the change on a long occasion and on a quick one (tile 11) differ by pauses of PE inside the down products of segment 0's mixed tiles, of which the quick one has none:

```profile
108.19 3.05 PE L554 MATMUL ps<-w_dn,hb 128*32 x40
```

```profile
106.56 2.34 PE L554 MATMUL ps<-w_dn,hb 128*32 x40
```

On the long one VectorE also starts on the logits of segment 2 0.7 us later against PE, and on their transpose 1.6 us later. These come to some 3 us in the change. Since one chip had both kinds of occasion (e5 to e8, and e12 to e15), the chip is not the cause; what is stays open, and there is no profile of the kernel before from a long occasion. Two profiles of two occasions must not be subtracted.

## Why the prediction missed

The ledger is 3.2 us over the sum of +1.5. The second scan alone is 3.3 off (+2.18 against -1.1), more than all other terms together: its step from VectorE's queue to the last add is the one that failed, and PE's clock, which the sum had left at full, is 1.7 of it.

**First scan: right.** -4.6 predicted, -4.36 measured on one occasion, tiles 6.85 apart, no wait at the mixed tiles; e10_old_shares shows that the spreading does it.

**Weights: the time was near, the mechanism half right.** The stream's late start was seen, and e1_late, whose `LATE` is the one of before, lands expert 7 at 86.1, the computed time. That is partly luck: the first transfer goes out at 43.76, 1.15 us later than before and not 2.05, and something else that the sum does not hold makes up for it. What failed is the sentence "That `LATE` sends experts 5 to 7 a tile sooner changes nothing in a queue that is full." It changed two things: the last weights land 1.7 sooner, and ScalarE, which issues them, stands 4.78 us in one issue, with PE's next copy behind it. I had counted the transfers and what waits for them, and not what waits behind the engine that issues them. The two places together are 4.35 by the ledger where 3.7 were forecast, which is luck in the sum: at tile 10, where the whole 3.7 was to be a wait for expert 7, weights hold PE for 0.57 in that trace (and for nothing in the one of 536.17), PE's own queue for 1.2, a term that the sum had at nothing, and ScalarE's issue costs the 2.29 at tile 8.

**Second scan: wrong sign.** Predicted -1.1 with a wait of 2.7 behind POOL; measured +0.5 without the clock's 1.7, with a wait of 4.51. The step that failed: "one more `hidden` (1.59) stands ahead of the last half state". What stands ahead of it is ScalarE's exponential, which the order puts behind the eviction of the tile's down product, that is behind PE itself. Once PE has to be through before the last half state can begin, exponential, scan, product and add follow one another in the open: 380.01 to 384.1.

**PE's clock: the rival of 0.13 came true, twice in the profiled run.** Its price was set at 2.2 a fall, half of the 4.3 us of slow filling at the start; a stretch of 3.41 us costs 1.7. I had tied it to one wait of 3.7; it came behind waits of 2.36 and 4.51, and e14_fill_nine shows by filling the second that it is the wait that does it. The Trainium skill, TensorE: Matmul & The Clock Gate, section on HAM oscillation, has an array that waits for DMA fall back to the low clock: the trace agrees, with a granted clock of 0.50 behind waits for ScalarE and POOL as well. This rival had deserved more than 0.13, since two of my own terms held waits near 3 us.

**Start: mis-sized.** +1.0 predicted, +0.21 measured. The wait of 1.25 behind VectorE's eviction came as computed (1.3), but the gates began at 11.07 and not at 12.29, which the sum left out; e7_cured_start finds the two starts alike.

**Ranks: right in size, wrong in cause.** +0.8 stood against +0.65. But e6_cured_ranks puts the ranks back and gains nothing: the bound is VectorE's work between the logits and the evictions.

**Router of segment 3: right in size, its cause untested.** +1.3 stood against +1.42. The prediction gave it to the transpose that comes four chunks later, and no run puts that back. The 1.42 are still there in the best version: from tile 49's down product to tile 51's it takes 409.06 - 393.94 = 15.12 us, the change 15.12, and the kernel before 13.70. So the logits of segment 3 at their old place are the next thing to try.

**The other rivals.** That the weights come in time, or that VectorE's waits are absent, is excluded by the rows above. That the scans gain less was right of the second, by another way than the one it named.

## What to carry to other kernels

A transfer is not free for the engine that issues it: with nine transfers of its queue on the way ScalarE stood in one issue for 4.5 to 5.1 us here, and all that was queued behind it was late; so spread issues out, or start the stream where the DMA engines have a gap. In a pipelined recurrence look at what the last piece waits for on every engine, not only on the one whose chain is longest: one piece put behind a tile's eviction cost 5.0 us here and one line mended it. And price a wait on PE of the length of those here (2.4 us and more) with a stretch at half clock behind it, 1.7 us.

## What the runs showed of the hardware that was not expected

- An issue of 640 KB takes 0.55 to 0.7 us as a rule. In all seven traces whose `LATE` sends experts 5 and 6 together, one takes 4.48 to 5.11: it begins with nine earlier transfers of its queue on the way and is let go with six.
- Of the thirteen waits of PE from 2.36 to 5.73 us in these traces ten had a granted clock of 0.50 behind them, for 3.41 us, and behind 4.51 three times (e1, e2, e10) for 6.83, which began while PE still waited; behind 2.39, 2.44 and 2.66 (and behind 2.05) it stayed full. e4's fall at 11.86 came behind two waits under 1 us. With it goes the spread: the changed kernel's own runs lie 3.6 to 5.4 us apart and e15's, with no wait over 1.4 behind the start, within 0.6.
- Ahead of the first mixed tile PE's queue takes 0.106 us for each of its waits, 0.50 for the load of a number from `table` and 0.47 for the address made from it; the exposed 1.2 us, or 0.70 with ten waits fewer, show as "issue".
